# The next batch's pre-activation moved to the start of its turn, into other banks and a second buffer, in the first three turns of a fused model kernel

## What is computed

```python
# per batch; h is (512, 64), n = 256, d = 64
x_update = relu(v_prev @ Dx.T)            # the pre-activation, 256 wide
x_t = 0.97 * x_state + x_update           # a recurrence over t
x_t = x_t / max(sum(|x_t|), 1e-12)
a_star = rho @ x_t
y_t = relu(ln(a_star) @ Dy.T) * relu(x_t)
v_star = ln(y_t @ E.T)
rho = 0.97 * rho + ln(v_prev)[:, None] * x_t[None, :]
h = h + v_star
h = h + experts(layernorm(h))             # top 2 of 8, gelu, 64 -> 128 -> 64
```

## Time and profile before

| | us |
|---|---|
| median of 3 runs | 782.51 (782.14 to 783.56) |
| the profiled execution, its own time | 784.06 |
| span in its profile | 782.2 |
| PE busy | 665.1 (85%) |
| DVE busy | 610.7 (78%) |
| ACT busy | 358.8 (46%) |
| POOL busy | 283.4 (36%) |

### The profile page before, as it was taken

One profiled execution on the slowest core, in us unless ns is written; L12 is line 12 of the kernel. 1 busy time (PEld: TensorE's weight loads), 2 busy tenths in 40 slices (PEclk: granted clock), 3 DMA queues, 4 the chain that ended last, 5 costly groups with the idle time before them and its releaser, 6 DMA issues.

```text
span 782.2 us, 16874 instructions
## 1 busy us (share of the span) xinstructions
PE 665.1 (85%) x4030; PEld 375.4 (48%) x4062; DVE 610.7 (78%) x2531; ACT 358.8 (46%) x819; POOL 283.4 (36%) x333
## 2 busy tenths in 40 slices
PE   2663993257799999999999999999999999999876
PEld 0552662134455555555555555555555555555432
DVE  5998887766778888888888888888888888887752
ACT  4000994002255555555554455555545554555543
POOL 1000000012234445555444444445555544444443
PEclk9999997568899999999999999999999999999988
DMA  7000000010333333333444433333333444432223
GB/s 243 31 0 0 1 0 11 4 60 28 87 104 90 89 88 88 88 89 89 106 104 101 111 104 88 88 88 88 88 89 88 103 103 105 107 108 62 62 62 75
DMA packets 45186, 61.06 MB, mean 78 GB/s; under 512 B 21560, under 2 KB 24108, under 8 KB 44652
## 3 DMA queue, kind: packets, MB, share of 16 engines
q1 hardware_dynamic: 43028, 60.13, 29.8%
q10 hardware_dynamic: 1944, 0.66, 0.4%
q0 software_dynamic: 192, 0.01, 0.0%
HBM read 55.77 MB, written 5.02 MB: 78 GB/s over the span
## 4 chain that ended last, share of the span: by engine, by line
PE 72%; DVE 12%; issue 6%; ACT 4%; POOL 2%; DMA 1%; DVEq 1%; SPq 0%; ACTq 0%; POOLq 0%
PE bank L1170 18%; PE bank L1268 13%; PE bank L1261 7%; PE bank L1262 6%; PE bank L1182 5%; PE bank L1209 5%; PE bank L1226 4%; PE bank L1286 3%; ACT skill_rows L511 3%; DVE same L667 3%; PE bank L1103 2%; PE bank L1114 1%; PE bank L1159 1%; PE bank L1218 1%; PE bank L1235 1%
## 5 line engine op out<-in xcount | busy, mean ns | idle before, releaser
L511 ACT ACTIVATE skill_rows<-bank,b1T,w_scale 128x512 f32<-128x512 f32 x256 | 194.6, 775 | 84.0 <-PE bank L1262 83.0
L1170 PE MATMUL bank<-feat_parts 128*128 128x256 f32 (+3 forms) x512 | 160.8, 449 | 4.7 <-DVE feat_parts L837 4.6
L1268 PE MATMUL bank<-skill_rows,w_sb 128*64 128x512 f32 x256 | 121.2, 594 | 0.2
L1269 PE MATMUL bank<-skill_rows,w_sb 128*64 128x512 f32 x256 | 121.2, 594 | 0.0
L1170 PEld LDWEIGHTS bank<-feat_parts 128*128 128x128 f32 x512 | 91.0, 194 | 47.1 <-issue 21.2
L387 POOL TENSOR_TENSOR t_z<-t_z,power 128x4 f32<-128x4 f32 x32 | 32.5, 1017 | 188.4 <-DVE t_z L884 188.4
L484 ACT ACTIVATE feat_parts<-bank 128x384 f32<-128x384 f32 (+2 forms) x96 | 36.8, 384 | 134.2 <-DVE feat_parts L843 134.2
L408 POOL TENSOR_TENSOR feat_parts<-skill_rows 128x512 f32<-128x512 f32 x64 | 81.3, 1270 | 17.9 <-DVE skill_rows L970 17.9
L375 POOL TENSOR_TENSOR same<-h_all,mean_h 128x256 f32 (+1 forms) x32 | 19.6, 612 | 164.5 <-DVEq L1034 164.4
L837 DVE TENSOR_TENSOR_SCAN feat_parts<-same,feat_parts 128x512 f32<-128x512 f32 x64 | 74.6, 1207 | 0.0
L393 POOL TENSOR_TENSOR h_scale<-t_h,power 128x4 f32<-128x4 f32 x32 | 32.6, 1018 | 109.7 <-DVE t_h L915 109.7
(11 more groups left out here) (252 smaller groups left out, 1286.8 us busy)
## 6 DMA issues: line engine op xcount, KB each, us to landing
same<-factor_d SPq DMA_DIRECT2D x32, 512.0 KB, 3.8
skill_rows<-w_d SPq DMA_DIRECT2D x32, 512.0 KB, 6.1
feat_parts<-w_d SPq DMA_DIRECT2D x32, 512.0 KB, 6.1
skill_rows<-skill_row_d SPq DMA_DIRECT2D x4, 1024.0 KB, 7.7
out<-o_sb SPq DMA_DIRECT2D x32, 128.0 KB, 6.3
w_sb<-in_L_ffn_W ACTq DMA_DIRECT2D x2, 256.0 KB
w_d<-wT SPq DMA_DIRECT2D x32, 16.0 KB, 1.4
table_k<-table_d SPq DMA_DIRECT2D x9, 2.5 KB
```

The lines of the kernel that those rows point to most:

```text
L511: act.activation(hid[:, e, :], h_bank[e % 2][:, :], ACT.Gelu, bias=b1T[:, e:e + 1], scale=w1_scale[:, e:e + 1]).then_inc(ac_gelu, 1)
L1170: last = pe.matmul(n_bank[sc % 2][:, 0:WIDE[sc]], xs[:, k, sc * P:(sc + 1) * P], xs[:, k, sc * P:S], start=(k == 0), stop=(k == NK - 1))
L1268: pe.matmul(z_bank[q % 2][0:D, :], w2_sb[:, 2 * q, :], hid[:, 2 * q, :], start=True, stop=True)
L1269: pe.matmul(z_bank[q % 2][D:P, :], w2_sb[:, 2 * q + 1, :], hid[:, 2 * q + 1, :], start=True, stop=True)\
```

## The change

In turns 0, 1 and 2 the pre-activation of batches 1, 2 and 3 is the turn's first work on PE, and goes into the `h_bank`; DVE's two relu operations for it are the first work of DVE's turn. DVE's two scans run ahead of the two gates of the turn, and for batches 1 and 3 they write `half` in place of `xs`. Scores and gates of those batches read there. New waits: the update waits for the relu operations of the batch before; scores 0 and 1 wait for the gates of the batch before; `hidden(0, 0)` and `hidden(0, 1)` for the relu operations of batch 3; POOL's `add_pairs` of batch 0 for the gates of batch 3. From turn 3 on the order is as it was.

```diff
--- before.py
+++ after.py
@@ -45,6 +45,7 @@
 WIDE = [S - P * sc for sc in range(C)]
 CAUSAL = OFF[-1] + WIDE[-1]
 GROUP = 8
+FILL = 3
 NG = J // GROUP
 EXP_MASK = 0x7F800000
 
@@ -251,6 +252,16 @@
 
             return ap.unsqueeze(2).to_broadcast([ap.shape[0], ap.shape[1], n])
 
+        def is_fill(b):
+
+            return isinstance(b, int) and 1 <= b <= FILL
+
+        def xs_of(b):
+            return half if is_fill(b) and b % 2 else xs
+
+        def pre_of(b):
+            return h_bank if is_fill(b) else n_bank
+
         def of_half(rows, half):
 
             chunks = rows.rearrange("p (c n) -> p c n", c=C)
@@ -405,6 +416,8 @@
 
                 pool.wait_ge(dv_tm, NP * b + 2 * n + 2)
                 wait(pool, po_acc, b)
+                if isinstance(b, int) and b == 0:
+                    pool.wait_ge(dv_y, 2 * NK * (FILL + 1))
                 pool.tensor_tensor(half[:, n, :], tm[:, 2 * n, :], tm[:, 2 * n + 1, :], ALU.add).then_inc(po_half, 1)
 
             def add_halves(b):
@@ -823,19 +836,27 @@
 
 
 
-            def scan(b):
+            def scan_relu(b):
 
                 dve.wait_ge(ld_factor, 16 * (b + 1))
-                wait(dve, pe_s, C * b)
-                wait(dve, dv_y, 2 * NK * b)
                 for k in range(NK):
                     dve.wait_ge(pe_pre, NK * b + k + 1)
-                    dve.scalar_tensor_tensor(relu_b[:, k, :], n_bank[k][:, :], 0.0, factor[:, 1, :], ALU.max, ALU.mult)\
-                       .then_inc(dv_relu, 1)
+                    dve.scalar_tensor_tensor(relu_b[:, k, :], pre_of(b)[k][:, :], 0.0, factor[:, 1, :],
+                                             ALU.max, ALU.mult).then_inc(dv_relu, 1)
+
+            def scan_run(b):
+
+                used = b - 1 if is_fill(b) else b
+                wait(dve, pe_s, C * used)
+                wait(dve, dv_y, 2 * NK * used)
                 for k in range(NK):
                     dve.wait_ge(dv_relu, NK * b + k + 1)
-                    dve.tensor_tensor_scan(xs[:, k, :], factor[:, 0, :], relu_b[:, k, :], 0.0, ALU.mult, ALU.add)\
+                    dve.tensor_tensor_scan(xs_of(b)[:, k, :], factor[:, 0, :], relu_b[:, k, :], 0.0, ALU.mult, ALU.add)\
                        .then_inc(dv_x, 1)
+
+            def scan(b):
+                scan_relu(b)
+                scan_run(b)
 
             def diagonal(b, sc):
                 dve.wait_ge(pe_s, C * b + sc + 1)
@@ -854,13 +875,13 @@
                 s.done(dve.tensor_tensor(t, st[:, :, 1], st[:, :, 4], ALU.subtract))
                 s.done(dve.tensor_tensor(w, st[:, :, 2], st[:, :, 5], ALU.add))
 
-            def gate(b, half):
-
-                dve.wait_ge(pe_y, 2 * b + half + 1)
+            def gate(b, n):
+
+                dve.wait_ge(pe_y, 2 * b + n + 1)
                 wait(dve, pe_zT, b)
-                core = n_bank[half][:, :].rearrange("p (k c n) -> p k c n", k=NK, c=2)
+                core = n_bank[n][:, :].rearrange("p (k c t) -> p k c t", k=NK, c=2)
                 for k in range(NK):
-                    dve.scalar_tensor_tensor(of_half(ys[:, k], half), core[:, k], 0.0, of_half(xs[:, k], half),
+                    dve.scalar_tensor_tensor(of_half(ys[:, k], n), core[:, k], 0.0, of_half(xs_of(b)[:, k], n),
                                              ALU.max, ALU.mult).then_inc(dv_y, 1)
 
             def z_stats(b, s):
@@ -976,6 +997,9 @@
                 r, t, k = i - 1, i - 2, i - 3
                 n = Steps(dve, res_steps, N_RES * r)
                 m = Steps(dve, mlp_steps, N_MLP * t)
+                early = is_fill(i + 1)
+                if early:
+                    scan_relu(i + 1)
                 if res:
                     z_stats(r, n)
                     z_halves(r, n)
@@ -1012,12 +1036,14 @@
                 if mlp:
                     weigh(k, 0, 1 - side)
                     weigh(k, 1, 1 - side)
+                if early:
+                    scan_run(i + 1)
                 if att:
                     gate(i, 0)
                     gate(i, 1)
                 if done:
                     finish(i - 4)
-                if ahead:
+                if ahead and not early:
                     scan(i + 1)
                 if mlp:
                     weigh(k, 2, 1 - side)
@@ -1155,20 +1181,26 @@
             def update(b):
 
                 for k in range(NK):
-                    wait(pe, dv_y, 2 * NK * b + NK * (k - 1))
-                    pe.matmul(n_bank[k][:, :], table_k[:, D + k * P:D + (k + 1) * P],
+                    if is_fill(b):
+                        pe.wait_ge(attn_w_in, 1)
+                        pe.wait_ge(dv_relu, NK * b)
+                    else:
+                        wait(pe, dv_y, 2 * NK * b + NK * (k - 1))
+                    pe.matmul(pre_of(b)[k][:, :], table_k[:, D + k * P:D + (k + 1) * P],
                               feat_k[:, bass.ds(b * S, S)], start=True, stop=True).then_inc(pe_pre, 1)
 
             def scores(b, sc):
 
                 if sc == 0:
                     pe.wait_ge(dv_x, NK * (b + 1))
+                if sc < 2 and is_fill(b):
+                    pe.wait_ge(dv_y, 2 * NK * b + NK * (sc - 1))
                 if sc >= 2:
                     pe.wait_ge(dv_diag, C * b + sc - 1)
                     pe.wait_ge(ac_off, (C - 1) * b + sc - 1)
                 for k in range(NK):
-                    last = pe.matmul(n_bank[sc % 2][:, 0:WIDE[sc]], xs[:, k, sc * P:(sc + 1) * P],
-                                     xs[:, k, sc * P:S], start=(k == 0), stop=(k == NK - 1))
+                    last = pe.matmul(n_bank[sc % 2][:, 0:WIDE[sc]], xs_of(b)[:, k, sc * P:(sc + 1) * P],
+                                     xs_of(b)[:, k, sc * P:S], start=(k == 0), stop=(k == NK - 1))
                 last.then_inc(pe_s, 1)
 
             def values(b):
@@ -1257,6 +1289,8 @@
 
             def hidden(b, e, side):
                 pe.wait_ge(ac_xT, b + 1)
+                if isinstance(b, int) and b == 0 and e < 2:
+                    pe.wait_ge(dv_relu, NK * (FILL + 1))
                 wait(pe, ac_gelu, E * b + e - 1)
                 pe.matmul(h_bank[e % 2][:, :], w1k[:, 0, e, :], xT[side][:], start=True, stop=False)
                 pe.matmul(h_bank[e % 2][:, :], w1k[:, 1, e, :], xT[side][:], start=False, stop=True).then_inc(pe_hid, 1)
@@ -1289,6 +1323,9 @@
 
             def turn(i, att, res, rt, mlp, done, ahead, side):
                 r, t, k = i - 1, i - 2, i - 3
+                early = is_fill(i + 1)
+                if early:
+                    update(i + 1)
                 if att:
                     scores(i, 0)
                 if mlp:
```

## The result

The changed kernel takes 786.89 us (median of six runs, 786.16 to 789.07), the kernel before 782.79 beside it (six runs, 782.11 to 783.56). The ratio is 1.005, 95% interval 1.0036 to 1.0064: slower by 4.1 us. Forecast were 782.6 and a range up to 784.7; both are missed.

A forecast was written before the change was run, and what follows sets the result against it. PE's own work was taken to cover most of the relu and scan chain, leaving waits of 0.15, 1.09 and 0. Terms +1.6 - 1.1 - 0.45 = +0.05 us gave 782.6 after the median's offset, range 780.1 to 784.7.

The forecast's parts named there:

- Turn 0, relu ahead of the diagonal, +1.3: Turn 0 on DVE: batch 1's relu delay the first diagonal and all that follows by 1.3 us.
- Rival 2: Turn 0: idle PE behind the relu costs the clock, 2.2 us slower, 784.8; chance 0.20, fourth case included where it adds.
- `z_out` directly behind the gate: Ends of turns 0 to 2 on PE: `z_out` follows the last gate directly; -0.4, -0.4 and -0.85 us.
- the first rival: Turn 0's tail and turn 1's scores keep the full clock: 2.3 us faster, 780.3; chance 0.24.
- The scans go into the idle time ahead of the gates; it costs 0: Turns 0 to 2 on DVE: the next batch's scans fit the idle time before the gates, cost 0.
- the forecast's 0.4 off: End of turn 1 on PE: with the update gone, `z_out` leaves 194.04 for about 193.65, -0.4 us.
- the fourth case: Scans ahead of the gates become the wait: 0.7 us at most in turn 2, 0.6 for turn 1's relu.
- `z_out` gains 0.85 behind the gates of turn 2: End of turn 2 on PE: `z_out` moves from 1.0 us after the gates' end to about 0.15, -0.85.
- the assumption that the clock's pattern stays: Turns 0 to 2: granted clock keeps its pattern; another pattern in 165 to 215 can move the end by 2.
- The third rival: The chain is right: relu and scans come off PE's path, 7.1 us less, 775.4; chance 0.02.
- a wait of 0.15: End of turn 0: PE's wait for the scan before batch 1's scores, since `z_rows` had to run anyway.
- Behind turn 3, 0: Turn 3 on: POOL's first sum of batch 0 waits for batch 3's gates; 0, without cover 1.3 at most.

The follow-up runs named there:

- w8_after: The changed kernel plus matmuls nobody reads in PE's waits of turns 0 to 2, twelve more in turn 0's hole; 781.58 us, ratio 0.9965.
- x_before_turn2: The kernel before plus ten matmuls nobody reads on PE in turn 2 alone; 783.74 us, ratio 1.0.
- w8_before: The kernel before plus matmuls nobody reads in PE's waits of turns 0 to 2, twelve more in turn 0's hole; 783.64 us, ratio 0.9999.
- e6: The changed kernel with scans moved back behind the gates and a second buffer of factors; 783.42 us, ratio 0.9993 against the kernel before.
- x_after_turn2: The changed kernel plus ten matmuls nobody reads on PE in turn 2 alone; 784.16 us, ratio 1.0008.
- e3: The changed kernel with PE's transposes of `x_p` moved behind `z_out`; 788.44 us, ratio 1.0059 against the kernel before.
- w7_mixed: Changed kernel, scans behind gates in turns 1 and 2, two factor buffers, batch 1's relu right before its scans, unread matmuls in PE's waits; 779.34 us, ratio 0.9945.

## Why the prediction was wrong, step by step

**Turn 0, relu ahead of the diagonal, +1.3: right.** On before's clock of events (less 0.71) the diagonal came at 171.7 and `values` at 174.6, forecast 171.9 and 174.9; aT 0 is 0.95 later, 1.2 in w8_after. Rival 2, which put a lost clock there, was wrong about the place: the clock rose at 172.25 and held. Its time, 784.8, is nearest to the measured one, but by luck.

**End of turn 0 and turn 1.** `z_out` directly behind the gate: right, twice over, since it ran at the full clock (1.08), as did the update (0.38) and the scores. Here the first rival happened, priced at 2.3 in all; turn 1 is 2.67 shorter. Had it been the whole story, the kernel would be faster.

**"The scans go into the idle time ahead of the gates; it costs 0": this is the first step that failed**, in turns 1 and 2. I measured the hole on DVE and asked only who waits for DVE. What runs on POOL in that hole was not asked. In turn 1 the scans put 0.9 on POOL's power, and from the gates' start to `z_out` it is 2.76 where it was 2.02 and where the forecast's 0.4 off would have given 1.62: 1.1 lost. In turn 2 the gates stand 1.49 behind `y_core`, where the fourth case allowed "0.7 at most": DVE is busy up to 207.17, so the scans start only 0.42 before `y_core`, and they are 0.8 longer beside POOL. Without that 0.8 the fourth case's 0.7 comes out. That `z_out` gains 0.85 behind the gates of turn 2 was right (1.45 from their start, 2.44 before), and is spent on this.

**The second step that failed is the assumption that the clock's pattern stays, and by size it is the larger.** The text named its condition (another pattern in 165 to 215 can move the end by 2) and gave the slower side of it 0.20, all in turn 0. From the first rise to turn 3, PE is busy 5.66 + 8.47 = 14.1 us at the low level, and was 6.06 + 5.92 = 12.0. Halving that difference would make the clock's part only 1.1. That is too little: in the kernel before part of the slow work is covered, because at the full clock PE would there wait for the scans (in x_before_turn2 1.22 ahead of the scores of batch 3, where the earlier trace rows has no wait). The profiles at a steady clock measure it better. From the first scan to aT 3 the changed kernel takes 62.32, and 55.97 in w8_after: the clock costs it 6.35. The kernel before takes 59.19, and 58.29 in w8_before, or 56.7 less the 1.6 of its last low stretch: 0.9 to 2.5. So the clock takes 3.9 to 5.5 us more than before, and the new order by itself gives 0.7 to 2.3. This compares one execution of each.

So the 1.1 and 1.5 of the first step are real waits, but at a steady clock the waits that the change takes away (1.53, 1.22 and 1.22, where the forecast read 0.15, 1.09 and 0) outweigh them. In the runs either remedy alone takes most of the 0.5% back: scans away from POOL (e6, 0.9993) and matmuls in turn 2 (x_after_turn2, 1.0008). That is what one would see if waits make the end of turn 2 thin and the thin end costs turn 3 its clock. That the waits are what makes the clock fall is argued from this, not shown. e3, which takes one of the waits away and in most runs keeps the low clock, speaks against its being that simple.

**The third rival** (the chain is right, 775.4) was rightly small, but the argument against it leaned on a wait of 0.15 that is 1.53 at the full clock.

**Behind turn 3, 0: right.** 469.46 against 469.39; the new wait of POOL's first sum costs nothing.

## What to carry to other kernels

Idle time of an engine is free only if what runs beside it on the engine that shares its port is free to wait too: before moving a two-input DVE operation on SBUF into a hole, list what POOL does in that hole and who waits for POOL. A wait read beside a low clock is not the wait that will be there when the clock is up; price such a wait at both levels. And where a kernel fills up slowly, judge a reordering of the start by its ratio over many runs, and by what it leaves to the first dense turn, not by the turn that was edited.

## What was not expected of the hardware

- POOL's operations beside scans: 0.61 to 1.43 (128x256) and 1.01 to 1.90 (the power on 128x4), and the scan pair 2.33 to 2.70 and 3.12. The smallest operation loses as much as a large one, 0.9 and 0.8, as it does if what it loses is waiting and not work.
- How far the phase of the clock moves a kernel whose start is thin: the kernel before spread over 5.9 us on one chip (780.29 at a mean granted clock of 0.968 to 786.15 at 0.955, 19 runs), and e6 over 8.4. w7_mixed, in whose profile the clock is up throughout the fill, spread over 1.2 (six runs), but w8_after, of which the same holds, over 3.2 (nine runs), so not all of the spread is the clock's.
- Matmuls that nobody reads are worth 0.85% in the changed kernel and nothing in the kernel before, though in the profile of the latter too they leave only one low stretch, of 3.25 us.
